# A head's q and k operands in 48 rows in place of 64, in an attention kernel with split float32 products

## The reference, cut to what matters

```python
qkv = xw @ qkv_w + qkv_b                 # xw: LayerNorm of x, padded to 14 x 14 windows
q, k, v = (qkv[0], qkv[1], qkv[2])       # each (windows * 12, 196, 16)
...
rel_h = jnp.einsum('bhwc,hkc->bhwk', rq, Rh)
rel_w = jnp.einsum('bhwc,wkc->bhwk', rq, Rw)
...
attn = jax.nn.softmax(scores, axis=-1)   # scores: q k^T * 16**-0.5 + rel_h + rel_w
o = jnp.einsum('bqk,bkd->bqd', attn, v)
```

## Time and profile before

| | before |
|---|---|
| median of 3 runs | 190.46 us (189.41 to 191.38) |
| profiled execution | 190.22 us, of which its span 188.4 us |
| TensorE busy | 175.3 us, 93% of the span |
| TensorE's weight loads | 153.3 us |
| VectorE, ScalarE, GpSimd busy | 112.9, 87.5, 65.7 us |
| mean granted TensorE clock | 0.991 |
| DMA | 12958 packets, 19.45 MB |

### The profile page before, as it was taken

How to read it: one execution, slowest core, us unless ns; L and a number is a source line. 1 busy time by engine, 2 the same in 40 slices (tenths; PEclk the granted TensorE clock), 3 DMA queues, 4 the chain that set the end, 5 groups by cost and what they waited for, 6 DMA issues and landing times.

```text
span 188.4 us, 4169 instructions
## 1 busy us (share of the span) xinstructions
PE 175.3 (93%) x1502; PEld 153.3 (81%) x1502; DVE 112.9 (60%) x303; ACT 87.5 (46%) x230; POOL 65.7 (35%) x120
## 2 busy tenths in 40 slices
PE   7999999997998797899999999999999999999892
PEld 7766996696786675788877996878999999789892
DVE  6729675598888677587755776520111466779532
ACT  3496554934387666587785204554100223071300
POOL 1633439936055456431999521900000000000000
PEclk9999999999699999999999999999999999999999
DMA  5791227976939999957051300000012170000015
GB/s 161 210 221 25 89 79 205 225 204 180 185 105 187 218 213 205 209 115 239 12 155 41 129 0 0 0 3 0 3 43 83 42 171 0 2 0 3 0 31 138
DMA packets 12958, 19.45 MB, mean 103 GB/s; under 512 B 5197, under 2 KB 9695, under 8 KB 12938
## 3 DMA queue, kind: packets, MB, share of 16 engines
q0 software_dynamic: 3392, 10.98, 24.4%
q1 hardware_dynamic: 8810, 7.75, 17.5%
q10 hardware_dynamic: 736, 0.46, 0.9%
HBM read 6.79 MB, written 1.57 MB: 44 GB/s over the span
## 4 chain that ended last, share of the span: by engine, by line
PE 70%; DMA 9%; DVE 7%; SPq 5%; ACT 3%; issue 2%; POOL 0%; ACTq 0%; DVEq 0%; POOLq 0%
PE bank L1632 9%; PE bank L1649 8%; PE bank L1406 6%; PE bank L1474 5%; PE bank L1667 4%; DMA qop<-arena 4%; PE bank L1392 3%; SPq L607 3%; PE bank L1381 3%; PE bank L1488 3%; PE bank L1600 3%; DMA q_last<-maxt 3%; PE bank L1659 3%; PE bank L1446 3%; DMA xt<-in_x_tok 2%
## 5 line engine op out<-in xcount | busy, mean ns | idle before, releaser
L1190 DVE TENSOR_REDUCE negmax<-bank 98x2 f32<-98x392 f32 (+1 forms) x72 | 34.7, 525 | 8.8 <-PE bank L1446 8.7
L1474 PE MATMUL bank<-qop,kop 128*98 128x196 f32 (+4 forms) x140 | 22.6, 262 | 0.1
L951 ACT ACTIVATE arena<-bank 98x392 f32<-98x392 f32 x48 | 21.2, 489 | 2.5 <-PE bank L1474 2.2
L1446 PE MATMUL bank<-kop,qop 126*98 126x196 f32 x80 | 16.4, 294 | 5.3 <-DMA qop<-arena 3.8
L1474 PEld LDWEIGHTS bank<-qop,kop 128*98 128x98 f32 (+4 forms) x140 | 18.8, 176 | 0.9 <-issue 0.9
L1632 PE MATMUL bank<-h2t,wf 96*128 96x512 f32 x72 | 17.4, 398 | 0.4 <-ACT h2t L978 0.4
L1446 PEld LDWEIGHTS bank<-kop,qop 126*98 126x98 f32 x80 | 11.1, 175 | 7.3 <-issue 5.7
L1632 PEld LDWEIGHTS bank<-h2t,wf 96*128 96x128 f32 x72 | 13.3, 188 | 3.9 <-issue 0.6
L1649 PE MATMUL bank<-wf,arena 128*128 128x192 f32 x96 | 15.8, 326 | 0.0
L1649 PEld LDWEIGHTS bank<-wf,arena 128*128 128x128 f32 x96 | 15.7, 190 | 0.1
L1269 DVE TENSOR_TENSOR arena<-bank,arena 128x384 f32<-128x384 f32 x4 | 2.2, 556 | 22.1 <-PE bank L1649 22.1
(11 more groups left out here) (172 smaller groups left out, 379.5 us busy)
## 6 DMA issues: line engine op xcount, KB each, us to landing
kop<-arena POOLq DMA_DIRECT2D x20, 173.0 KB, 5.5
qop<-arena POOLq DMA_DIRECT2D x10, 227.5 KB, 6.7
qop<-arena SPq DMA_DIRECT2D x10, 130.0 KB, 2.5
qop<-arena POOLq DMA_DIRECT2D x10, 130.0 KB, 6.0
arena<-in_relw SPq DMA_DIRECT2D x2, 441.0 KB, 5.1
xt<-in_x_tok SPq DMA_DIRECT2D x4, 192.0 KB, 3.5
scratch<-arena SPq DMA_DIRECT2D x4, 192.0 KB, 2.0
k_last<-arena POOLq DMA_DIRECT2D x4, 173.0 KB, 4.8
```

The lines of the kernel that those rows point to most:

```text
L951: nc.scalar.activation(pg[:, e], src[0:HWIN, 0:2 * WIN], ACT.Exp, scale=HD ** -0.5).then_inc(emptied(key), 1)
L1190: nc.vector.tensor_reduce(negmax[0:rows, n % 2, at:at + cols], ps(key)[0:rows, 0:cols * width].rearrange("p (t k) -> p t k", t=cols), AX.X ...
L1446: ins = mm(ps(key)[0:HWIN, WIN * t:WIN * t + WIN], qo(h)[0:126, c0:c0 + HWIN], ko(h)[0:126, WIN * u:WIN * u + WIN], start=True, stop=True)
L1474: ins = mm(ps(key)[0:rows, at:at + n], ko(h)[:, c0:c0 + rows], rhs, start=True, stop=True)
```

## The change

A q slot keeps rows 0 to 31 (rounded q, twice over), and its rows 32 to 47 hold low q once. A k slot keeps rows 0 to 31, and its rows 32 to 47 hold rounded k once. The product of the two low parts is left out. Rows 48 to 63 of every slot are zeros, written once: GpSimd clears 16 rows inside `k2` (they belong to heads 6 to 11, whose low k is not written until later), and two DMAs copy these into the five slots of `kop` and of `qop`; the sixth slot takes its zeros from slot 0, in two DMAs ahead of the one for its mask rows. TensorE's instructions are the same in number and shape.

```diff
+        blank = k2[0:16, 1, 1]
...
         def q_rows(h, part):
             f, j = h // HH, h % HH
-            src = q2[j:j + HH * (HD - 1) + 1:HH, f, part, None, :].to_broadcast([HD, 2, QN])
-            return raw(qo(h)[32 * part:32 * part + 32]), raw(src)
+            if part == 0:
+                src = q2[j:j + HH * (HD - 1) + 1:HH, f, 0, None, :].to_broadcast([HD, 2, QN])
+                return raw(qo(h)[0:32]), raw(src)
+            return raw(qo(h)[32:48]), raw(q2[j:j + HH * (HD - 1) + 1:HH, f, 1, :])
...
             sp.dma_start(relw[:, 1], a["relw"][:, 1]).then_inc(relw_in[1], 16)
+
+            sp.wait_ge(blank_set, 1)
+            sp.dma_start(raw(kop[48:64]), raw(blank[:, None, :].to_broadcast([16, OWN, KN]))).then_inc(blank_in, 16)
+            sp.dma_start(raw(qop[48:64]), raw(blank[:, None, 0:QN].to_broadcast([16, OWN, QN]))).then_inc(blank_in, 16)
...
                     sp.dma_start(raw(k_last[64:128, :]), raw(kop[64:128, 0])).then_inc(krows_set[OWN], 16)
+                    sp.dma_start(raw(k_last[48:64, :]), raw(kop[48:64, 0])).then_inc(krows_set[OWN], 16)
+                    sp.dma_start(raw(q_last[48:64, :]), raw(qop[48:64, 0])).then_inc(qrows_copied, 16)
                     sp.dma_start(raw(q_last[120:126, :]), raw(qop[120:126, 0])).then_inc(qrows_copied, 16)
...
             nc.gpsimd.memset(raw(q2[:, 1, 1, QB + 112:QR]), 0.0).then_inc(set_up, 1)
+            nc.gpsimd.memset(raw(blank), 0.0).then_inc(blank_set, 1)
...
-                for copy in range(2):
-                    pool.dma_start(raw(ko(h)[32 * copy:32 * copy + 32]),
-                                   raw(k2[j:j + HH * (HD - 1) + 1:HH, f])).then_inc(k_loaded[h % NOK], 16)
+                pool.dma_start(raw(ko(h)[0:32]),
+                               raw(k2[j:j + HH * (HD - 1) + 1:HH, f])).then_inc(k_loaded[h % NOK], 16)
+                pool.dma_start(raw(ko(h)[32:48]),
+                               raw(k2[j:j + HH * (HD - 1) + 1:HH, f, 0])).then_inc(k_loaded[h % NOK], 16)
...
-                            pe.wait_ge(qrows_copied, 32)
+                            pe.wait_ge(qrows_copied, 48)
...
-                        pe.wait_ge(krows_set[h % NOK], 16 if h % NOK == OWN else 1)
+                        pe.wait_ge(krows_set[h % NOK], 32 if h % NOK == OWN else 1)
...
             pe.wait_ge(qrows_copied, 16)
+            pe.wait_ge(blank_in, 32)
```

More of the change, by code:

```diff
@@ L449, in build @@
         qrows_copied = sem("qrows_copied")
+        blank_set = sem("blank_set")
+        blank_in = sem("blank_in")
         krows_set = [sem(f"krows_set{i}") for i in range(NOK)]
```

## The result

The changed kernel takes 201.2 us in the median of 6 runs (200.15 to 203.38), the kernel before 190.38 us in 6 runs (188.19 to 191.41). The ratio is 1.061, with a 95% interval of 1.052 to 1.070: slower by 10.8 us. Some executions of any kernel here fall into a slower state: medians and ranges count all runs, ratios and their intervals only those outside that state. The profiled execution took 200.64 us, its span is 198.7 us (188.4 before) and the mean granted clock 0.957 (0.991 before).

The account below looks back on a forecast made before the run. TensorE, busy for 93% of the span, was taken to bound the kernel. From 190.22 us, -1.9 (waits in the loop) + 3.1 (`bv` late) + 0.8 (clock) gave 192.2 us, range 187.2 to 194.0.

Parts of the forecast that it names:

- `bv` is held back by the first zero copy: At the start, `bv` waits for the zero copy issued 0.4 us ahead; TensorE then stands still 3.1 us.
- The rival in which `bv` is not held back: At the start, `bv` loses at most 1.1 us, absorbed by TensorE's cover: 188.3 us; chance 0.27.
- How late: At the start, `bv` lands 4.2 us later, at 19.0 us, leaving TensorE idle 3.1 us.
- The clock: After TensorE's idle time at the start, a lowered clock costs 0.8 us, between 0 and 1.7.
- The gain in the loop: In the loop of heads, smaller q and k copies cut TensorE's `qop` waits by 1.9 us, between 0 and 3.8.
- What I put at nothing: GpSimd's clearing, zero copies running until about 22 us, two more copies before head 5: 0, up to 1 us in range.

Follow-up runs that it names:

- run 2: The kernel before plus only the clearing and two early zero copies, with first q and k loads waiting for them: 201.59 us.
- run 5: The changed kernel with the zero copy into `qop` moved behind `bv`, the one into `kop` left early: 201.15 us, one run.
- run 1: The changed kernel with both zero copies issued later, behind the mask copy and a wait for `bv`: 192.03 us, ratio 0.989.
- run 6: The changed kernel with `bv` issued by SyncE ahead of the early zero copies, in place of GpSimd: 190.68 us, ratio 0.991.
- run 3: The changed kernel with 14 dummy matmul passes on zeros where TensorE would stand still ahead of the last k product: 195.83 us.
- run 4: run 1 with the 16 narrow rows on every second row of the 32 and zeros between them: 187.02 us, ratio 0.975.
- run 7: run 6 with the row layout of run 4, 16 rows spread over 32: 187.05 us, ratio 0.972.
- run 8: The kernel before, second q and k copies from head 6 on moving only half their columns in all 32 rows: 187.03 us, ratio 0.973.

## Why the prediction was wrong

It said 192.2 us, within 187.2 to 194.0. By its own steps:

- **`bv` is held back by the first zero copy: right.** L1124 waits for `bv`, and `bv` lands near that copy. Run 2 shows that the zero copies alone do it, run 5 that the first is enough, runs 1 and 6 that either order which puts `bv` ahead cures it. The second copy seems to add some 1 us when it is issued almost with `bv` (21.1 in runs 2 and 3, 20.0 without it in run 5). The rival in which `bv` is not held back, and with it the Trainium skill's rule that each DMA engine goes round its queues packet by packet ("DMA: Bandwidth & Descriptors", Queues, rings and completion order), did not come true here: 96 KB on an otherwise empty queue landed 11.1 us after its issue.
- **How late: a little short.** I had 4.2 us and it was 5.6: the second half of `relw` landed 1.0 us later (7.2 us after its issue, against the 6.2 of the earlier trace rows), and the first zero copy was slower than I took it. TensorE's idle time was 3.63 in place of 3.1.
- **The clock: this step failed.** "I take 0.8, between 0 and 1.7" had its upper end from a stretch with short waits for VectorE. The clock cost 6.5 us, nearly four times that end. The nearest rows that I had were idle times of 1.0 and 1.55 us; here it was one of 3.63, over twice as long as any, and I bounded its price by theirs. The trace of before has no row of that kind, and the range ought to have said that it had no upper end there. Run 3 shows it was the idle time: with the array kept busy, head 0 was late by what the last product was late, and the span 3.6 us longer. In one of run 2's four executions the full fall can't have come, so even the right size would have been a range.
- **The gain in the loop: wrong choice between right ends.** I worked out that a copy's rate goes by the rows that it covers, which makes the gain 0, and then took 1.9, because its neighbours in the queue could fill what a narrow copy leaves. The neighbours filled nothing that TensorE could feel: the DMA share stays at 0.99 to 1.11 while 16-row copies run, and the waits are the old 3.8 us. The share of 0.34 around the single 6-row copy of the earlier trace rows says nothing of room in a full queue.
- **What I put at nothing was nothing.** GpSimd's clearing took 1.24 us beside other work. The zero copies were long in (22.5) when head 0 began. The two more copies ahead of head 5 delayed nobody: TensorE has no wait for `k_last` or `q_last`. Even the landing of the zero copies was near: about 22 forecast, 20.9 and 22.5 measured.

The terms as measured: loop 0, `bv` 3.8, clock 6.5, together +10.3 on a profiled execution of 190.22, so 200.5; it took 200.64. Of the miss of 9 us against the median, the clock is 5.7, the loop 1.9, the idle time 0.7; the rest is the difference between runs. The ends of the forecast's terms (gain 1.0 to 3.0, `bv` 2.5 to 4.0, clock 0 to 1.7) add up to 189.7 to 194.9 and not to the 190.4 to 194.0 given for them; neither reaches 200. The rate from 60 to 80 us before was 203 to 219 GB/s, not 209 to 219, which changes no term.

What made runs 4, 7 and 8 fast agrees with the other page that was weighed, "SBUF — State Buffer" of the Trainium skill (Door 1: The DMA port swizzle): 16 adjacent partitions reach 4 of 16 ports. By its formula every second one of 32 partitions reaches the same 8 as all 32 do. The runs show the rates and waits; the ports themselves no row shows.

Three things stay open. The changed kernel has a second fall of the clock at 120 to 125 us (0.70, with PE busy 5.00 of 5 us), the kernel before one at 45 to 55 us, runs 1 and 6 none in their profiles. They cost 1.7 us each and nothing here says what starts them. Then the ratios: they put runs 4, 7 and 8 some 5 us below before, where the waits account for some 2.9, and runs 1 and 6 some 2 us below, where the waits account for 0.4 at most. Some 2 us are thus common to all of them. Falls of the clock in the kernel before may be a part; a small gain from the fewer bytes in runs 1 and 6 isn't ruled out, and there is no trace of before from these two groups. And runs 5 and 2 stay low for longer than the changed kernel (0.54 and 0.69 in 35 to 40 us), after idle times of 3.23 and 4.50 us, so the length of the fall doesn't simply go with that of the idle time.

## What to carry to other kernels

A small load that the next step waits for goes out before bulk copies with time to spare, whatever queue these are on: 0.5 us in the order of issue was worth 4.4 us of landing here. An idle time of TensorE is not priced by its length once it is longer than those that the trace shows to be free: here a lateness of 3.8 us cost 10.3. And a copy within SBUF that is made smaller should lose columns or every second row, not half of an adjacent block of rows: the same bytes took 2.9 us off the waits one way and nothing the other.

## What was not expected of the hardware

- A granted clock of 0.50 held for over 10 us of PE busy without a gap, after 3.63 us idle (and after 3.23 and 4.50 in runs 5 and 2), while an idle time of 1.19 us behind matmuls on zeros in run 3 left it at 1.00.
- DMA engines at a share of 1.03 that carry 118 GB/s (15 to 20 us after, mostly copies into 16 adjacent rows), and at 0.92 carry 205 (run 4, every second row): the share tells that the engines are occupied, not that they move much.
